# A bucket sort by matrix products: other weights, a turned sum, and a share of the products on ScalarE

## Time and profile before

| | |
|---|---|
| time, median of 3 runs | 9809.44 us (9801.89 to 9814.32) |
| the profiled execution | 9807.02 us, span 9805.2 us |
| PE busy | 8923.7 us, 91% |
| DVE busy | 7921.7 us, 81% |
| ACT busy | 7321.4 us, 75% |
| POOL busy | 6810.7 us, 69% |
| the sort's loop | from about 70 to 780 us |

### The profile page before, as it was taken

The page is one execution under the profiler, slowest core; times in us unless marked ns, Lnnn a source line. Parts: engine busy times, 40 slices in busy tenths (PEclk is TensorE's granted clock), DMA queues, the critical chain, the costliest instruction groups (busy, mean ns, idle before and its releaser), DMA issues.

```text
span 9805.2 us, 277571 instructions
## 1 busy us (share of the span) xinstructions
PE 8923.7 (91%) x65693; PEld 7235.6 (74%) x65693; DVE 7921.7 (81%) x33650; ACT 7321.4 (75%) x23591; POOL 6810.7 (69%) x7059
## 2 busy tenths in 40 slices
PE   7996777777776999999997999999997999999997
PEld 6985666666664777777775777777775777777775
DVE  7898999999997777777775777777775777777775
ACT  2204999999996777777775777777775777777775
POOL 1336777777775777777775777777775777777775
PEclk9998999999997999999998999999998999999998
DMA  2003444444444555555556555555556555555556
GB/s 49 5 12 82 108 109 109 109 109 109 109 109 115 159 159 159 159 159 158 159 159 133 158 160 160 157 159 159 159 159 140 159 159 159 159 159 159 159 159 122
DMA packets 1133743, 1308.57 MB, mean 133 GB/s; under 512 B 452629, under 2 KB 847723, under 8 KB 1133325
## 3 DMA queue, kind: packets, MB, share of 16 engines
q1 hardware_dynamic: 899446, 841.26, 28.0%
q0 software_dynamic: 229008, 460.45, 21.1%
q10 hardware_dynamic: 5126, 4.76, 0.2%
HBM read 1041.61 MB, written 260.45 MB: 133 GB/s over the span
## 4 chain that ended last, share of the span: by engine, by line
PE 63%; DMA 10%; DVE 9%; issue 8%; POOL 7%; ACT 3%; SPq 1%; DVEq 0%; POOLq 0%; ACTq 0%
PE bank L737 52%; DMA agg<-agg_d,arena 6%; POOL agg L705 6%; PE bank L897 5%; PE bank L882 5%; PE bank L850 2%; DMA agg<-feat_d,arena 2%; DVE agg L1545 2%; DVE agg L1555 2%; ACT arena L1011 2%; DVE arena L1535 1%; POOL wide L718 1%; DMA arena<-type_d 1%; DVE arena L1513 1%; DVE arena L1504 0%
## 5 line engine op out<-in xcount | busy, mean ns | idle before, releaser
L705 POOL DMA_INDIRECT agg<-agg_d,arena x5124 | 4852.1, 947 | 1731.1 <-issue 1432.1
L1655 DVE TENSOR_TENSOR arena<-agg,bank 128x256 f32<-128x256 f32 x2562 | 1080.2, 422 | 1451.1 <-PE bank L737 1064.4
L705 POOL DMA_INDIRECT agg<-feat_d,arena x1708 | 1618.3, 947 | 529.4 <-issue 421.4
L737 PE MATMUL bank<-arena 128*128 128x129 f32 x10248 | 1825.6, 300 | 32.6 <-ACT arena L1090 30.5
L737 PE MATMUL bank<-tmp,wide 128*128 128x256 f32 x5124 | 1540.1, 383 | 10.1 <-DMA wide<-left_d 10.1
L737 PE MATMUL bank<-tmp,kw_s 128*128 128x256 f32 x5124 | 1532.9, 381 | 0.0
L737 PEld LDWEIGHTS bank<-arena 128*128 128x128 f32 x10248 | 1338.5, 190 | 211.3 <-issue 43.3
L1086 ACT ACTIVATE arena<-arena 128x1 f32<-128x1 f32 x2562 | 754.6, 295 | 931.7 <-DVE arena L1519 890.6
L1081 ACT ACTIVATE arena<-agg,arena 128x256 f32<-128x256 f32 x2562 | 1337.9, 522 | 57.8 <-DVE arena L1648 52.2
L1094 ACT ACTIVATE tmp<-bank 128x256 f32<-128x256 f32 x2562 | 982.1, 383 | 427.6 <-PE bank L737 372.6
L1648 DVE CUSTOM_DVE_ANT_0 agg<-bank,arena 128x256 f32<-128x256 f32 x2562 | 1228.6, 480 | 19.6 <-issue 8.0
(11 more groups left out here) (242 smaller groups left out, 17251.0 us busy)
## 6 DMA issues: line engine op xcount, KB each, us to landing
state_d<-arena SPq DMA_DIRECT2D x488, 455.0 KB, 2.7
arena<-key_d SPq DMA_DIRECT2D x489, 448.0 KB
arena<-type_d SPq DMA_DIRECT2D x367, 448.0 KB
wide<-left_d SPq DMA_DIRECT2D x2562, 64.0 KB
agg<-agg_d,arena POOLq DMA_INDIRECT x5124
agg<-feat_d,arena POOLq DMA_INDIRECT x1708
arena<-er_d SPq DMA_DIRECT2D x854, 1.0 KB
arena<-peers SPq DMA_DIRECT2D x489, 7.0 KB
```

Source lines behind the costliest of these rows:

```text
L705: nc.gpsimd.indirect_dma_start(out=rows_r[:, k % R, c, 0:width], out_offset=None, in_=table, in_offset=bass.IndirectOffsetOnAxis(ap=peer_r ...
L737: return nc.tensor.matmul(out, lhsT, rhs, start=start, stop=stop)
L1655: V.tensor_tensor(val_r[:, j % R, :, 0:F], rows_r[:, j % R, :, 0:F], bank[0][:, 0:G].rearrange("p (c f) -> p c f", c=2), ALU.mult).then_in ...
```

## The change: slot one-hots become the weights

- `gather_runs(n)`: 13 products instead of 26. `slot_hot` (64 columns) is now the weights, both payload halves of `carried` together (98 columns) the moving side. The sum lies in bank 4+h with the 64 slots on partitions.
- ScalarE copies that sum to SBUF (`summed`, `sum_copied`), and a new `turn_runs(n)` on TensorE transposes its two halves into another part of the bank (`run_turned`), one pass after `gather_runs(n)`: the order is rank(n), gather_runs(n-1), turn_runs(n-2), and the loop has one pass more.
- ScalarE's loop, pass n: wait for the gather of n, copy its sum, `copy_run(n-1)` (the old L963, which now waits for `run_turned`), `carry_share(n+2)`, and the pass over `dst_block` where there is one.
- `carry(n)` on VectorE makes 10 of the 13 columns; `carry_share(n)` on ScalarE makes the other 3, as six activations of 49 columns each. `spread(n)` waits for the share of n-2, since both read the same `block_hot` buffer.
- VectorE's wait for `run_stored` and the two slots of `run_at` are as before.

```diff
+SHARE = 3
+TURN_AT = P
@@ TensorE
                 pe.wait_ge(slots_made, n + 1)
+                pe.wait_ge(share_carried, n + 1)
                 if n >= 2:
                     pe.wait_ge(run_copied, n - 1)
+                for c in range(SC):
+                    last = mm(bank[4 + h][0:CAP, 0:2 * NB], slot_hot[:, h, c, :], carried[:, h, c, :, :].rearrange("p j n -> p (j n)"), c == 0, c == SC - 1)
+                last.then_inc(run_summed, 1)
+
+            def turn_runs(n):
+
+                h = n % 2
+                pe.wait_ge(sum_copied, n + 1)
                 for j in range(2):
-                    for c in range(SC):
-                        last = mm(bank[4 + h][0:NB, j * CAP:(j + 1) * CAP], carried[:, h, c, j, :], slot_hot[:, h, c, :], c == 0, c == SC - 1)
-                last.then_inc(run_summed, 1)
+                    last = nc.tensor.transpose(bank[4 + h][0:NB, TURN_AT + j * CAP:TURN_AT + (j + 1) * CAP], summed[:, h, j, :], ident[0:CAP, 0:CAP])
+                last.then_inc(run_turned, 1)
...
-            for n in range(CHUNKS + 1):
+            for n in range(CHUNKS + 2):
                 if n < CHUNKS:
...
                     rank(n)
-                if n >= 1:
+                if 1 <= n <= CHUNKS:
                     gather_runs(n - 1)
+                if n >= 2:
+                    turn_runs(n - 2)
@@ ScalarE
-            for n in range(CHUNKS):
-                act.wait_ge(run_summed, n + 1)
+            def carry_share(n):
+
+                h = n % 2
+                act.wait_ge(hot_made, n + 1)
+                if n >= 2:
+                    act.wait_ge(run_summed, n - 1)
+                for c in range(SHARE):
+                    for j in range(2):
+                        last = nc.scalar.activation(carried[:, h, c, j, :], block_hot[:, h, c, :], ACT.Identity,
+                                                    scale=payload[:, n * SC + c, j:j + 1], bias=nought[:, 0:1])
+                last.then_inc(share_carried, 1)
+
+            def copy_run(n):
+
+                act.wait_ge(run_turned, n + 1)
                 if n >= 4:
                     act.wait_ge(run_stored, 16 * (n - 3))
...
+            carry_share(0)
+            carry_share(1)
+            for n in range(CHUNKS):
+                act.wait_ge(run_summed, n + 1)
+                if n >= 2:
+                    act.wait_ge(run_turned, n - 1)
+                nc.scalar.copy(summed[:, n % 2, :, :].rearrange("p j n -> p (j n)"), bank[4 + n % 2][0:CAP, 0:2 * NB]).then_inc(sum_copied, 1)
+                if n >= 1:
+                    copy_run(n - 1)
+                if n + 2 < CHUNKS:
+                    carry_share(n + 2)
...
+            copy_run(CHUNKS - 1)
@@ VectorE, spread(n) and carry(n)
                     dve.wait_ge(run_sized, n - 1)
+                    dve.wait_ge(share_carried, n - 1)
...
-                V.tensor_tensor(carried[:, h, :, :, :], block_hot[:, h, :, :].rearrange("p c (o n) -> p c o n", o=1).to_broadcast([P, SC, 2, NB]),
-                                payload[:, c, :].rearrange("p c (j o) -> p c j o", o=1).to_broadcast([P, SC, 2, NB]), ALU.mult)
+                V.tensor_tensor(carried[:, h, SHARE:, :, :],
+                                block_hot[:, h, SHARE:, :].rearrange("p c (o n) -> p c o n", o=1).to_broadcast([P, SC - SHARE, 2, NB]),
+                                payload[:, n * SC + SHARE:(n + 1) * SC, :].rearrange("p c (j o) -> p c j o", o=1).to_broadcast([P, SC - SHARE, 2, NB]), ALU.mult)
```

More of the change, by code:

```diff
@@ L239, in gnn_kernel @@
         carried = agg_flat[:, 0:4 * SC * NB].rearrange("p (a c j n) -> p a c j n", a=2, c=SC, j=2)
+        summed = agg_flat[0:CAP, 4 * SC * NB + 4 * CAP:4 * SC * NB + 4 * CAP + 4 * NB].rearrange("p (a j n) -> p a j n", a=2, j=2)
+        nought = sb("nought", [P, 1])
         runs = agg_flat[0:NB, 4 * SC * NB:4 * SC * NB + 4 * CAP].rearrange("p (a n) -> p a n", a=4).bitcast(I32)
@@ L314, in gnn_kernel @@
         run_summed = sem("run_summed")
+        sum_copied = sem("sum_copied")
+        run_turned = sem("run_turned")
+        share_carried = sem("share_carried")
         run_sized = sem("run_sized")
@@ L963, in _ @@
                 nc.scalar.copy(runs[:, n % 4, :].bitcast(U16).rearrange("p (s j) -> p j s", j=2),
-                               bank[4 + n % 2][0:NB, 0:2 * CAP].rearrange("p (j s) -> p j s", j=2)).then_inc(run_copied, 1)
+                               bank[4 + n % 2][0:NB, TURN_AT:TURN_AT + 2 * CAP].rearrange("p (j s) -> p j s", j=2)).then_inc(run_copied, 1)
+            carry_share(0)
[9 more added lines that the diff above has]
+                    carry_share(n + 2)
                 b = n - SIGNS_AT
@@ L1152, in _ @@
             V.memset(xs[:, NB - 1, :], 0.0)
+            V.memset(nought[:], 0.0)
             V.memset(wx[:], 0.0).then_inc(pads_set, 1)
@@ L1385, in carry @@
             def carry(n):
-                h, c = n % 2, slice(n * SC, (n + 1) * SC)
+                h = n % 2
                 dve.wait_ge(hot_made, n + 1)
```

## The result

The changed kernel takes 10001.1 us (median; 9991.7 to 10008.8) against 9805.7 us for the kernel before on the same chip: a ratio of 1.020, with a 95% interval of 1.0188 to 1.0212, slower by 195 us. The profiled execution has a span of 9997.9 us, 192.7 more than before. Forecast was 9960, range 9925 to 10070. In the code of after, L1469 is the old L1423 (`run_at`), L1472 the old L1426 (`slot_hot`), L1436 the old L1391 (`carry`), L1460, L1427 and L1465 the masking, `spread` and the reduction, L744 is `mm`, L782 the turn, L1002 the copy of the sum, L993 the copy of the run, L984 ScalarE's share, L573 the store.

What follows compares the result with a forecast made beforehand. TensorE bounds the old sort; the store loop bounds the changed one at 6.79 us a pass, 1.22 over 5.571. Over 121 passes that is +147.5 us, +150 in all on 9807.02, median 2.4 higher: 9960 us, range 9925 to 10070.

Steps and rivals of the forecast that it cites:

- main step: Sort loop: the store comes one pass later under VectorE's unchanged wait, so its path has one pass; cycle 6.79 us.
- The gather: TensorE's gather in the sort: 26 instructions of 98 columns at 0.0865 us, 2.25 us in all, 0.81 less.
- The turn: Two f32 transposes of 64 columns on TensorE in the sort: 0.11 us (0 to 0.22).
- The short store: GpSimd's store in the sort starts beside VectorE's reduction only, takes 0.95 us and lands in 2.3 (2.1 to 3.0).
- The rule cited: Whichever starts first, a two-input VectorE operation or GpSimd, holds the shared SBUF port and the other one blocks.
- Rival B: Sort: the store starts while `spread` still runs; landing 3.0 us, cycle 7.49, total 10043 us; chance 11%.
- The slack before: Old sort: the path from `run_at` to landing and the next `run_at` takes 8.05 of 11.02 us, so it hides.
- Rival D: Sort: TensorE's clock falls to half through its pauses; cycle 9.1 us, +432 us, total 10240 us; chance 4%.
- late stores: Sort: stores landing late as in the earlier trace put the cycle at 7.2 us, total 10010 us.
- C: Sort: the gather gains nothing and stays at 3.06 us; cycle 7.60 us, total 10057 us; chance 5%.
- Rival A: Sort: the store loop doesn't bind and TensorE's own 4.81 us is the cycle; -85 us, total 9725 us; chance 6%.
- The parts at nothing: Sort: ScalarE's added work, at most 4.9 us a chunk in all, hides; VectorE's wait for the share costs nothing.

Runs made afterwards that it cites:

- e7: The changed kernel with `run_at` in three slots instead of two, VectorE waiting for the store of chunk n-3: 9752.9 us, ratio to the kernel before 0.9948.
- e3: The kernel before, with VectorE waiting for the store of chunk n-1, not n-2, before it writes `run_at`: 10063.9 us, ratio 1.026.
- e1: The changed kernel with `run_at` in four slots instead of two, VectorE waiting for the store of chunk n-4: 9749.7 us, ratio to the kernel before 0.994.
- e4: The changed kernel with 12 more unread bf16 products of 196 columns at the end of each rank: 10012.4 us, ratio to the kernel before 1.021.
- e8: The changed kernel with 12 more unread bf16 products of 128 columns ahead of each rank: 9989.6 us, ratio to the kernel before 1.0188.
- e5: The changed kernel with four `run_at` slots, but without ScalarE's share and the waits for it: 9754.2 us, ratio to the kernel before 0.9955.
- e6: The kernel before with ScalarE's share alone (3 of 13 columns), old gather and two slots: 9804.6 us, ratio 1.0004.

## Why the prediction was right

*The loop.* The prediction's main step, that store(n-1) follows `run_at`(n) and must land before `run_at`(n+1), is shown: giving the path one pass more takes 248 us away (e7), and taking one away from the kernel before costs 258 us (e3).

*Its terms.* Forecast and measured in a plain pass: `run_at` to gather 1.20 and 1.20; gather to the copy of the sum 2.35 and 2.45; to the copy of the run 0.25 and 0.24; to the store 0.60 and 0.60; store to `run_at` 2.39 and 2.26. Together 6.79 and 6.75 (median 6.73). The gather was put a little too low: the 26 instructions take 2.34 till the turn starts, 0.090 each and not the 0.0865 of the line between 64 and 256 columns. The turn takes 0.24 us of TensorE's time in e1, from 405.82 to the next rank at 406.06, and not 0.11 or the 0.22 at most. (In the pass of after shown above the rank comes 0.28 behind the turn's start, but there it waits for `spread`, which ends at 409.37.) The turn is hidden in after; in e1, where TensorE bounds, turn and gather together make the cycle 5.02 and not 4.81.

*Landing.* The short store came true. The row of after has GpSimd at 0.95 us, begun under the reduction, and a median landing of 2.1. The rule cited, of the Trainium skill ("SBUF — State Buffer", section "SBUF: two separate sides"), agrees: in e1 the store starts at 406.76 under the two-input product, which ends at 407.80, and takes 1.86 us, till 0.82 behind that end. Rival B (7.49) did not come.

*The slack before.* The prediction gives the path of before 8.05 of the 11.02 us of two passes, with the gather 1.20 behind `run_at`. That is the path as after a stall. In the running sort the gather stood behind the next rank and started 3.44 behind `run_at`, and the median from `run_at` to the landing was 10.15 us. So 0.8 us were left, not 3, and 12 landings between 160 and 760 us came too late. The conclusion for the changed kernel doesn't rest on it.

*The size.* Of the 195 us, 150 were forecast. In the cycle, 6.73 for 6.79 saved 7 us; about 33 us came from the clock, 4 from planning that held the rank up, and 10.5 from late landings. The step that was mis-sized is the one that let TensorE run at full clock in the forecast: "Rival D" had it fall in every pass or in none. It fell in 22 of 121, a part of D on top of the forecast. That 10001 still lies under the 10010 of the forecast's own span is in part luck: that room was put there for late stores, which took 10.5 us of it, and the clock took some 33 that the forecast had at nothing. The room above it, up to 10070, was for B and C, and neither came. The row to go by, 77% busy at 1.00, is a mean over a stage; it says nothing of how the pauses lie. In the sort every plain pass has one of about 1 us, and some with planning have one of 1.8 to 3.3. The late landings were known from the earlier trace rows and were put into the range only.

The Trainium skill ("TensorE: Matmul & The Clock Gate", section "What's actually happening") makes activity what lifts the clock and half rate the default. The traces agree with the direction: 0.95 with pauses, 0.98 and 0.99 with filling (e4, e8), 1.00 in e1 from 300 to 460 us.

*Rival A* (the loop doesn't bind, TensorE's cycle decides, 9725) is what the change gives with one slot more: 9750, at TensorE's 5.02 us.

*The parts at nothing.* ScalarE's share was put at no cost and no gain, and e5 and e6 show no difference clear of the noise either way. It takes 2.01 us in the pass shown, under the 2.5 used as an upper end.

## What to carry to other kernels

When a step of a pipeline is put off by one pass, list every wait that counts passes of what comes out of it, the small buffers that nobody thinks of included: here 49 x 2 words cost 250 us, more than four times what the change was worth. A wait that shows up in only 12 of some 108 passes is the sign of a loop with little slack; add up its path as it runs, queues included, and compare it with the passes it has, before anything is moved. Work taken off an engine that waits for another, as the share here, was worth nothing clear of the noise (e5, e6).

## What the runs showed of the hardware that was not expected

The granted clock of TensorE fell in single passes of a loop in which it is busy 79% of the time, in some behind a pause of 1.8 us or more, in others behind no more than the 1.0 and 0.4 us that every pass has; a gather then takes up to 4.06 us, not 2.41. Work that nobody reads, 12 products a pass, 0.7 us together, made the loop 10.6 us shorter ahead of the rank (e8); 1.2 us of it behind the rank left it 13 us longer (e4), though slow gathers became fewer in both.

Two f32 transposes of 64 columns hold TensorE for 0.24 us (e1), when two of 128 columns in a stream of other work take 0.22. Why half the columns save nothing was not tried.
